# Four edits around the first two lists of a four-layer graph network: scans that write a wider tile, a clearing moved behind the first indices, weight blocks and counts moved beside a gather, and other column counts for a row gather

## The reference, cut to what matters

```python
def _L0_gnn_ref(feat, src, dst):                  # first layer, K = 10, ALPHA = 0.1
    ...
    def step(f, _):
        f = f * src_norm[:, None]
        agg = jax.ops.segment_sum(f[src], dst, num_segments=n)
        f = agg * dst_norm[:, None]
        f = (1.0 - ALPHA) * f + ALPHA * feat0
        return (f, None)
    feat, _ = jax.lax.scan(step, feat, None, length=K)
    return feat
...
x = _layernorm(x + _L0_gnn_ref(x, src, dst), axis=-1)
x = _layernorm(x + _L1_gnn_ref(x, edge_index, ...), axis=-1)      # attention with 4 heads
x = _layernorm(x + _L2_gnn_ref(x, ..., src, dst, edge_type_86), axis=-1)   # relation weights
x = _layernorm(x + _L3_gnn_ref(x, edge_weight, edge_index, 100000), axis=-1)
```

## Time and profile before

| what | us |
|---|---|
| time, median of 3 runs (2603.21 to 2606.65) | 2606.37 |
| the profiled execution: its own time | 2606.76 |
| its span, from the first to the last instruction | 2605.0 |
| DVE busy in it (73%) | 1897.5 |
| POOL busy in it (66%) | 1725.1 |
| ACT busy in it (23%) | 602.2 |
| PE busy in it (20%) | 523.0 |

### The profile page before, as it was taken

One profiled execution on the slowest core, in us unless ns is written; L12 is line 12 of the kernel. 1 busy time (PEld: TensorE's weight loads), 2 busy tenths in 40 slices (PEclk: granted clock), 3 DMA queues, 4 the chain that ended last, 5 costly groups with the idle time before them and its releaser, 6 DMA issues.

```text
span 2605.0 us, 24407 instructions
## 1 busy us (share of the span) xinstructions
PE 523.0 (20%) x3579; PEld 334.4 (13%) x3579; DVE 1897.5 (73%) x3483; ACT 602.2 (23%) x1410; POOL 1725.1 (66%) x1741
## 2 busy tenths in 40 slices
PE   5771000077000000000000303520036553000000
PEld 2340000067000000000000302420013221000000
DVE  7776888888863566552899847608989999888871
ACT  7992333133000000000010302631235441200000
POOL 6777767777747766655575767676366670575776
PEclk9995555589555555555555656555556555555555
DMA  7002333200013123221222120111100000210000
GB/s 241 13 12 78 97 98 97 66 14 13 11 64 15 31 21 22 29 26 17 109 24 71 21 64 11 9 30 52 54 8 8 9 9 1 67 16 7 10 10 9
DMA packets 101760, 101.70 MB, mean 39 GB/s; under 512 B 58264, under 2 KB 92744, under 8 KB 99920
## 3 DMA queue, kind: packets, MB, share of 16 engines
q0 software_dynamic: 53664, 20.91, 9.1%
q1 hardware_dynamic: 47728, 80.16, 8.6%
q10 hardware_dynamic: 320, 0.20, 0.0%
HBM read 38.06 MB, written 60.81 MB: 38 GB/s over the span
## 4 chain that ended last, share of the span: by engine, by line
DVE 35%; issue 23%; POOL 16%; DMA 11%; DVEq 3%; PE 2%; ACT 1%; POOLq 1%; SPq 1%; ACTq 0%
POOL ring L763 6%; POOL cring L471 4%; POOL out_dram L898 2%; DMA cring<-sums_by_list,cidx 2%; POOL attention_by_edge L863 2%; DMA ring<-YW 2%; POOL ring L856 2%; DMA cring<-sums_by_edge,cidx 1%; DVE RB L1217 1%; DVE banks L1098 1%; DVE banks L1088 1%; DVE SW L1094 1%; DVE SW L1103 1%; DVE SW L1093 1%; DVE SW L1341 1%
## 5 line engine op out<-in xcount | busy, mean ns | idle before, releaser
L480 POOL DMA_INDIRECT XS<-in_x_dram,xsi x196 | 199.6, 1018 | 70.2 <-issue 62.4
L480 POOL DMA_INDIRECT SW<-node_table,srci x196 | 200.4, 1022 | 65.9 <-issue 65.9
L480 POOL DMA_INDIRECT XD<-in_x_dram,xdi x196 | 195.0, 995 | 62.7 <-issue 62.7
L898 POOL DMA_INDIRECT out_dram<-ring,ridx x168 | 175.6, 1045 | 72.8 <-issue 50.4
L471 POOL DMA_INDIRECT cring<-sums_by_list,cidx x128 | 123.8, 967 | 85.1 <-issue 75.4
L882 POOL DMA_INDIRECT out_dram<-z4w,oidx x112 | 111.9, 999 | 86.4 <-ACT oidx L2479 53.3
L2556 PE MATMUL banks<-YW 128*128 128x392 f16 x784 | 139.9, 332 | 45.7 <-ACT YW L2298 45.0
L2638 PE MATMUL banks<-tl,dcar 128*128 128x32 f32 (+1 forms) x14 | 4.4, 405 | 700.2 <-DVEq L1330 523.3
L763 POOL DMA_INDIRECT ring<-x_by_edge,aidx x96 | 102.4, 1066 | 49.3 <-issue 44.7
L763 POOL DMA_INDIRECT ring<-rgcn_table,aidx x56 | 56.3, 1006 | 102.7 <-DMA aidx<-rows 85.7
L1001 DVE TENSOR_SCALAR YW<-YW,b_d 128x784 f16<-128x784 f16 x196 | 82.7, 422 | 46.6 <-PE banks L2556 44.7
(11 more groups left out here) (621 smaller groups left out, 3273.2 us busy)
## 6 DMA issues: line engine op xcount, KB each, us to landing
SW<-in_x_dram SPq DMA_DIRECT2D x20, 625.0 KB
out_dram<-SW SPq DMA_DIRECT2D x20, 625.0 KB
sums_by_list<-RB SPq DMA_DIRECT2D x2, 1800.0 KB
sums_by_edge<-RB SPq DMA_DIRECT2D x1, 3528.0 KB, 9.8
sums_by_list<-RB SPq DMA_DIRECT2D x2, 1600.0 KB
XS<-in_x_dram,xsi POOLq DMA_INDIRECT x196
list_values_by_edge<-RB SPq DMA_DIRECT2D x1, 3136.0 KB
attention_by_edge<-RB SPq DMA_DIRECT2D x1, 3136.0 KB
```

Of the source, the lines that this page charges most:

```text
L480: pool.indirect_dma_start(out=dest[:, t * w:(t + 1) * w], out_offset=None, in_=table, in_offset=bass.IndirectOffsetOnAxis(ap=idx[:, t:t + ...
L898: pool.indirect_dma_start(out=out[:, :], out_offset=bass.IndirectOffsetOnAxis(ap=index(j), axis=0), in_=row(j), in_offset=None, bounds_che ...
```

## The change

1. **The sums go straight into the wide tile.** The 32 scans of the first step and the carry behind them write `FULL` (36 numbers from column to column) in place of `S` (32), and the copy of `S` into `FULL` is gone.
2. **The first indices of list 0 go ahead of the clearing.** The wait for `s_fullw` and the two clearings become the `between` of list 0's `list_gather`.
3. **Weight blocks and target counts move into the `between` of the payload's gather.** `make_list` comes ahead of them, and so do the first two requests. On PE the transpose that `make_list` asks for (`column_row(7)`) moves ahead of the two carries of the counts.
4. **Other column counts of XD on POOL:** 162, 22 and 12 columns in place of 148, 38 and 10.

```diff
-        XS_AHEAD, XD_EARLY, XD_MID = 160, 148, 186
+        XS_AHEAD, XD_EARLY, XD_MID = 160, 162, 184
...
-            sums_of_dst = lambda src3, dst3, flat: segment_sums(src3, dst3, D, dmask, dfirst,
-                                                                enter=lambda first: carry_run(flat, first))
+            sums_of_dst = lambda src3, dst3, flat, w=D: segment_sums(src3, dst3, D, dmask, dfirst,
+                                                                     enter=lambda first: carry_run(flat, first, w))
...
-            sums_of_dst(Y3, S3, S)
+            sums_of_dst(Y3, FULL[:, :, 0:D], RB[:, 0:T * TW], TW)
...
-            st.do(V.tensor_copy(FULL[:, :, 0:D], S3))
...
-            dve.wait_ge(s_fullw, 16)
-            st.do(V.memset(zr[:, :, :], 0.0))
-            st.do(V.memset(RB[:, 0:CW * TW], 0.0))
-            st.wait()
-            list_gather(0, cs, 0, lidx2, row_take(0, cs, TW, RB[:, 0:CW * TW], TW, YW, True), 9)
+            st.wait()
+
+            def clear_sums():
+
+                dve.wait_ge(s_fullw, 16)
+                st.do(V.memset(zr[:, :, :], 0.0))
+                st.do(V.memset(RB[:, 0:CW * TW], 0.0))
+                st.wait()
+
+            list_gather(0, cs, 0, lidx2, row_take(0, cs, TW, RB[:, 0:CW * TW], TW, YW, True), 9, clear_sums)
...
+            cs = make_list(1, t1w, CW, pb[:, 0:1], float(CW - ZROW))
+
+            def weights_and_counts():
+
...
-            dve.sem_inc(s_sri, 1)
-            cs = make_list(1, t1w, CW, pb[:, 0:1], float(CW - ZROW))
-            list_gather(1, cs, 0, lq, pay_take(1, cs), 1)
+                dve.sem_inc(s_wb, 1)
...
+                dve.sem_inc(s_sri, 1)
+
+            list_gather(1, cs, 0, lq, pay_take(1, cs), 1, weights_and_counts)
...
+            column_row(7)
             carry(dcar, 1)
             carry(dbak, 1)
-            column_row(7)
```

More of the change, by code:

```diff
@@ L1748, in _ @@
-            st.seq(V.tensor_tensor(relf[:, NB:RW], relf[:, NB:RW], b_b2[:, :], ALU.add))
-            st.seq(V.tensor_copy(rel3[:, 0, :], relf[:, :]))
-            for k in range(2):
-                st.seq(V.tensor_tensor(relf[:, :], relf[:, :], rel3[:, k, :], ALU.subtract))
-                st.seq(V.tensor_copy(rel3[:, k + 1, :], relf[:, :]))
-            st.wait()
-            dve.sem_inc(s_wb, 1)
-            ones_t = ones[:, 0:1].to_broadcast([P, T]).unsqueeze(2)
-            segment_sums(ones_t, c3[:, :].unsqueeze(2), 1, dmask, dfirst)
@@ L1759, in _ @@
-            spread_back(c3[:, :].unsqueeze(2), 1, dend, dstf)
-            dve.sem_inc(s_sri, 1)
-            cs = make_list(1, t1w, CW, pb[:, 0:1], float(CW - ZROW))
-            list_gather(1, cs, 0, lq, pay_take(1, cs), 1)
+            cs = make_list(1, t1w, CW, pb[:, 0:1], float(CW - ZROW))
+            def weights_and_counts():
+                for k in range(2):
+                    st.seq(V.tensor_tensor(prod[:, 0:NH * D].rearrange("p (h o) -> p h o", h=NH),
+                                           wcat[:, :].rearrange("p (h o) -> p h o", h=NH),
+                                           mid(wsd[:, k * D:(k + 1) * D], NH), ALU.mult))
+                    st.seq(V.tensor_reduce(ua[:, k, :], prod[:, 0:NH * D].rearrange("p (h o) -> p h o", h=NH), AX.X,
+                                           ALU.add))
+                for k in range(2):
+                    for h in range(NH):
+                        m = (k * NH + h) * D
+                        st.do(V.tensor_scalar(udiag[:, m:m + D], ident[0:D, 0:D], ua[0:D, k, h:h + 1], None, ALU.mult))
+                for j in range(GT):
+                    r = slice(32 * j, 32 * j + 32)
+                    st.do(V.tensor_scalar(bd1[r, j * NH * D:(j + 1) * NH * D].rearrange("i (o h) -> i o h", h=NH),
+                                          wcat[r, :].rearrange("i (h o) -> i o h", h=NH), 1.0 / NH, None, ALU.mult))
+                    st.wait()
+                    st.do(V.tensor_reduce(bdm[r, j * D:(j + 1) * D], bd1[r, j * NH * D:(j + 1) * NH * D].rearrange(
+                        "i (o h) -> i o h", h=NH), AX.X, ALU.add))
+                    for part, w in ((w16[r, 0:NB * D].rearrange("i (o b) -> i o b", b=NB),
+                                     wf[r, :].rearrange("i (b o) -> i o b", b=NB)),
+                                    (w16[r, NB * D:(NB + 1) * D], aw[r, 0:D]),
+                                    (w16[r, (NB + 1) * D:(NB + 2) * D], aw[r, 2 * D:3 * D])):
+                        st.seq(V.tensor_copy(part, w))
+                        if j >= 2:
+                            st.seq(V.tensor_tensor(part, w, part, ALU.subtract))
+                    st.do(V.tensor_copy(bdy[r, j * D:(j + 1) * D], aw[r, D:2 * D]))
+                st.seq(V.tensor_tensor(relf[:, NB:RW], relf[:, NB:RW], b_b2[:, :], ALU.add))
+                st.seq(V.tensor_copy(rel3[:, 0, :], relf[:, :]))
+                for k in range(2):
+                    st.seq(V.tensor_tensor(relf[:, :], relf[:, :], rel3[:, k, :], ALU.subtract))
+                    st.seq(V.tensor_copy(rel3[:, k + 1, :], relf[:, :]))
+                st.wait()
+                dve.sem_inc(s_wb, 1)
+                ones_t = ones[:, 0:1].to_broadcast([P, T]).unsqueeze(2)
+                segment_sums(ones_t, c3[:, :].unsqueeze(2), 1, dmask, dfirst)
+                spread_back(c3[:, :].unsqueeze(2), 1, dend, dstf)
+                dve.sem_inc(s_sri, 1)
```

24 lines of the change are left out of this document (removed).

## The result

The changed kernel takes 2591.08 us, the median of four runs (2589.12 to 2591.61), beside 2606.51 us for the kernel before (four runs, 2603.21 to 2609.08): a ratio of 0.994, 95% interval 0.9925 to 0.9955. The profiled execution is one of 2591.61 us with a span of 2589.9 us. 15.3 us were forecast as the gain, 15.4 were measured.

A forecast was written before the change was run, and what follows sets the result against it. No engine bounds the kernel throughout; the gain is what leaves the chain between 709 and 950 us. Terms 7.3 + 8.0 = 15.3 us off 2606.37 give 2591 us; range 2587 to 2599, by the terms' bounds 2589 to 2592.5.

The forecast's parts named there:

- First term: Ahead of list 0: POOL starts list 0 at 755.5 rather than 762.78, 7.3 us gained (bounds 6.6 to 8.3).
- reading the trip count: Ahead of list 0, POOL reads the trip count into a register: nothing to about 0.9 us, taken as 0.5.
- doubling: Rival ahead of list 0: the table's write doubles beside the gathers, first term 1.7 us, time 2597; chance 0.05.
- The copy and the scans: Ahead of list 0: dropping the copy moves DVE up 3.35 us; the scans' step of 36 costs 0.
- 4 us of cover: Ahead of list 0: about 4 us by which the table, landing at 750.6, precedes the end of POOL's columns.
- The clearing: List 0's sums, cleared behind the table's landing: costed at 0; rival that it holds POOL, 2598 us, chance 0.06.
- Weights and counts: At the payload: swapped with make_list and the requests, they run beside the first gathers, 9.0 us gained.
- Two trips, one covered, one hand-over: At the payload: one of two gather trips goes beside weights and counts, less one hand-over; 9.0 us gained.
- some 8 us of POOL idle: Sign at the payload: POOL idles some 8 us ahead of the second trip of gathers.
- POOL late by 1 us at list 1: Ahead of list 1: with 12 columns of XD instead of 10, POOL is about 1 us late, starting at 911.2.
- Second term: Payload to list 1: list 1's start moves from 919.15 to 911.2, 8.0 us gained (bounds 7.5 to 9.0).
- Behind 950 us: Nothing changes there but line numbers; rival that a later wait takes the gain back, 2606 us, chance 0.06.

The follow-up runs named there:

- the second profile: The changed kernel, unchanged, run again beside c1: 2589.63 us, ratio 0.9934 to the kernel before.
- a4: Changed kernel with the old shares of XD's columns (148, 38 and 10): 2590.14 us, ratio 0.9938 to the kernel before.
- b3: Kernel before with one edit alone, list 0's requests ahead of the table wait and the clearing: 2598.32 us, ratio 0.9970.
- a1: Changed kernel with the scans writing S again and the 3.43 us copy into the wide tile back: 2590.38 us, ratio 0.9939 to the kernel before.
- a3: Changed kernel with weight blocks and counts back ahead of make_list, PE's transposition back behind its carries: 2594.64 us, ratio 0.9960 to the kernel before.
- c1: Changed kernel with 160, 30 and 6 columns of XD in place of 162, 22 and 12: 2584.45 us, run again 2586.33 us.
- b1: Kernel before with make_list and the payload's requests ahead of weights and counts, old column shares: 2602.85 us, ratio 0.9989.
- b2: Kernel before with one edit alone, the 32 scans writing the wide tile without the copy: 2603.85 us, ratio 0.9990.
- a2: Changed kernel with the table wait and the clearing of list 0's sums back ahead of the requests: 2594.01 us, ratio 0.9953 to the kernel before.
- d1: c1 with DVE's clearing of S moved into its idle time ahead of the table's landing: 2581.31 us, ratio 0.9896 to the kernel before.

## Why the prediction was right

**First term, 7.3 forecast, 8.07 measured** (list 0's first gather 53.51 to 45.44 us behind line 1668; 8.10 in the second profile), inside its bounds of 6.6 to 8.3. What was said to end last did: POOL's columns, with the table landed 3.06 us ahead of list 0 (752.76 to 755.82). Two sizes were off, both on the dear side. The 0.5 us for reading the trip count, for which no row stood, isn't there: list 0's first gather follows the last column by 1.26 us, as any other follows the one before. And a column took 1.25 us, as the quickest row said, and not 1.28. The write beside 14 more gathers took 10.7 us from issue to landing in place of 9.8, far from doubling (its row in the page's list of DMA issues):

```profile
sums_by_edge<-RB SPq DMA_DIRECT2D x1, 3528.0 KB, 10.7
```

**The copy and the scans.** The scans kept 538 ns. Of the 4 us of cover about 2.2 were left: where POOL waits for the table (a4, b3), list 0 starts 0.87 to 0.88 us behind DVE's first row after the landing, so here it could have started at 753.64 in place of 755.82. What the prediction did not see is that leaving the copy out paid only by making room for the columns (b3 has nearly the same place with the copy), and that with them the copy would have cost about as much by POOL as by the table: it would have held one gather (a1). It also took the 14 early columns as a given cost and asked only whether they fit; they cost 3.12 us at list 0 (a4).

**The clearing** cost 0: gathers of 0.94 to 0.95 us beside it, as beside the other clearing.

**Weights and counts, 9.0 forecast at the payload.** From list 0's last take (840.37 before, 832.14 after) to the payload's last take it is 66.76 us before and 58.14 after, 8.62 less. a3 undoes the swap alone and loses 8.43 by list 1. Two trips, one covered, one hand-over: the second trip's gathers start at 878.19, 1.31 us behind DVE's first take, where 1.27 were reckoned. What was mis-sized is the way into the loop: from the end of the counts to the first take it took 0.92 us (875.96 to 876.88) and not 0.35. The sign "some 8 us of POOL idle" came out as 12.61; by the prediction's own times, eight gathers from 864 on and the second trip at 886.0, 12 follow.

**POOL late by 1 us at list 1**, measured 0.8 to 1.0: its start moved from 0.75 us behind DVE's requests to 1.56, and from 12.02 us behind the payload's last take to 13.02. c1 with six columns there takes this wait away.

**Second term, 8.0 forecast, 8.89 measured** (list 0's start to list 1's: 156.37 to 147.48; 147.09 in the second profile). The difference is a piece that the prediction has not: from list 0's first gather to its last take 77.59 us passed before and 76.32 after, 1.27 less. Taken to the first instruction of line 1594, behind the last take, it is 80.9 to 81.4 us in the five kernels with the old shares of columns (before, a4, b1, b2, b3) and 79.9 to 80.2 in the eight profiles with new shares and that line (after twice, a1, a2, a3, c1 twice, d1). So about 1 us goes with the shares. The traces show where it lies: through ten of list 0's fourteen rounds of four gathers the take starts 2.5 to 2.9 us behind the start of the fourth gather, and in the last four it starts 3.35, 5.45, 7.88 and 8.17 us behind it before and 3.34, 4.91, 6.52 and 7.29 after. Of the 1.27 us, 0.88 are in the last of these rounds; the other 0.39 are POOL's last gather, which came that much later before, since the late landings held DVE's requests up. Why these transfers land late, and later with the old shares, no run shows; it stays open.

**Behind 950 us** nothing was given back beyond the scatter: 1685.85 us before, 1686.60 and 1682.86 after. The two terms came out at 17.0 together, 1.7 above the forecast; in the first profile the scatter of the parts outside the stretch took 1.9 of it away, so that the time agreed better than the terms did. That 15.4 measured stand so close to 15.3 forecast is luck. The medians of 15.4 and 17.5 us gained (2606.51 less 2591.08, 2607.09 less 2589.63) show how far it could have come out otherwise. By its own terms the lower gain of 14.1 us ends at 2592.3 and not at the 2592.5 written, which changes nothing.

## What to carry to other kernels

What an edit is worth depends on the others that are in: build the sum of the parts only for the engine that ends last once all of them are in, and look where two of them cancel, as the missing copy (3.36 us) and the 14 early columns (3.12 us) did here. When requests can go out ahead of a wait that they don't need, that alone may be the whole gain; and work that only has to be done at some time goes first into a stretch in which its own engine waits, not over to an engine that shares something with it. For edits of a tenth of a per cent, compare places counted from a common instruction, since whole times of the same kernel scatter by more.

## What the runs showed of the hardware that had not been expected

- Small operations on VectorE were held by a clearing on GpSimd to its end: eight scalings of 32x32 took 5.69 us beside a 5.34 us clearing, 1.27 without it. The other way round, a clearing on DVE left GpSimd's gathers alone (0.95 us beside 5.29 and 6.06 us), while a 3.43 us copy stretched one to 3.79 and a 6.69 us product one to 6.72.
- Both large clearings on DVE have idle time ahead of them that waits for nothing in the profile, 1.25 us ahead of 5.29 and 1.45 ahead of 6.06, and it moved with the clearing (749.32 in d1_clear_early). Length and idle time together are 6.54 us for 6272 numbers on a partition and 7.51 for 7200, 1.04 ns a number both times: the idle time grows with the size, and counts with the instruction.
- Whole times of one kernel lie up to 4.7 us apart, and two profiles of the same kernel differ by 3.74 us in the 1685 us behind list 1's start, in small pieces at several places. Their cause stays open.
- The last rounds of list 0 land late in every kernel here: a take starts up to 7.3 us behind the start of its fourth gather in the changed kernel and 8.2 in the one before, where 2.5 to 2.9 are usual.
